# Graph network with two residual layers on one core: another order of the preparation, fewer rows gathered ahead, and other queues and store sizes in the last stage

## The reference

```python
msg_in = concat([x[src], edge_attr], -1)             # 400,000 x 192
h = relu(msg_in @ W1.T + b1)
messages = h @ W2.T + b2
agg = segment_sum(messages, dst)                     # 12,500 x 128
# a GRU cell with agg as its input and x as its state
r, z = sigmoid(i_r + h_r), sigmoid(i_z + h_z)
n = tanh(i_n + r * h_n)
x = layernorm(x + (1 - z) * n + z * x)
# second layer: mean over the edges in the other direction
agg = segment_sum(x[dst], src);  deg = segment_sum(1, src)
x = layernorm(x + agg / max(deg, 1) @ weight + x @ root_weight + bias)
```

## Time and profile before

| | us |
|---|---|
| median of 3 runs | 4435.34 (4431.68 to 4440.71) |
| the profiled execution | 4442.85 |
| its span | 4441.0 |
| PE busy | 3928.3 (88%) |
| POOL busy | 3013.7 (68%) |
| DVE busy | 2906.7 (65%) |
| ACT busy | 2353.3 (53%) |

### The profile page before, as it was taken

One profiled execution on the slowest core, in us unless ns is written; L12 is line 12 of the kernel. 1 busy time (PEld: TensorE's weight loads), 2 busy tenths in 40 slices (PEclk: granted clock), 3 DMA queues, 4 the chain that ended last, 5 costly groups with the idle time before them and its releaser, 6 DMA issues.

```text
span 4441.0 us, 106931 instructions
## 1 busy us (share of the span) xinstructions
PE 3928.3 (88%) x39936; PEld 3633.4 (82%) x39936; DVE 2906.7 (65%) x7270; ACT 2353.3 (53%) x4278; POOL 3013.7 (68%) x3198
## 2 busy tenths in 40 slices
PE   6488999988989898999999998989898999989875
PEld 6377888887979797988888897979797888879775
DVE  4465667666666676666666666667676676766644
ACT  2165555555555555555555555555555555555633
POOL 1677777777777777777777777777777777777600
PEclk9587999999999999989999998999999999999989
DMA  7455888797969697978879796969798887979655
GB/s 216 87 173 159 231 232 248 219 260 212 268 192 287 200 272 212 254 218 235 242 221 257 216 269 194 283 199 277 212 257 225 234 242 224 265 211 273 193 169 167
DMA packets 1017822, 999.82 MB, mean 225 GB/s; under 512 B 204167, under 2 KB 857548, under 8 KB 1016921
## 3 DMA queue, kind: packets, MB, share of 16 engines
q1 hardware_dynamic: 830878, 459.88, 40.3%
q10 hardware_dynamic: 84075, 321.56, 21.2%
q0 software_dynamic: 102352, 211.43, 18.4%
HBM read 655.22 MB, written 337.22 MB: 223 GB/s over the span
## 4 chain that ended last, share of the span: by engine, by line
PE 69%; DMA 7%; DVE 7%; ACT 4%; issue 3%; SPq 3%; POOL 2%; DVEq 1%; ACTq 0%; POOLq 0%
PE stream_pse L1193 15%; PE stream_psa L1202 13%; PE stream_pse L1185 13%; PE stream_psw L1209 10%; PE stream_psw L1208 10%; DMA ring<-in_ea_blocks_dram 5%; PE stream_psw L1246 2%; ACT stream_a_sb L893 2%; SPq L749 2%; PE stream_psw L1247 2%; POOL ring L838 2%; PE stream_psw L1248 2%; DVE stream_col L978 1%; ACT stream_hid L855 1%; DMA ring<-r 1%
## 5 line engine op out<-in xcount | busy, mean ns | idle before, releaser
L838 POOL DMA_INDIRECT ring<-y,ring x2480 | 2349.6, 947 | 842.9 <-issue 728.9
L893 ACT CAST stream_a_sb<-stream_psa 98x512 f16<-98x512 f32 x3125 | 1770.5, 586 | 1508.5 <-PE stream_psa L1202 1468.2
L1202 PE MATMUL stream_psa<-stream_col,stream_row 128*98 128x256 f16 x6250 | 1145.2, 284 | 157.2 <-ACT stream_a_sb L893 125.8
L1208 PE MATMUL stream_psw<-stream_z,stream_strip 128*128 128x129 f16 x9060 | 1255.3, 221 | 14.1 <-issue 6.9
L1209 PE MATMUL stream_psw<-stream_z,stream_strip 128*128 128x128 f16 x9060 | 1260.9, 221 | 0.0
L1193 PE MATMUL stream_pse<-w1b,ring 128*128 128x128 f32 x6250 | 1037.2, 300 | 79.1 <-DVE stream_tiny L1105 32.7
L956 DVE TENSOR_TENSOR ring<-stream_pse,ring 128x384 f32<-128x384 f32 x1000 | 489.3, 489 | 830.4 <-PE stream_pse L1193 745.9
L978 DVE TENSOR_TENSOR stream_col<-stream_ramp,stream_twin 128x1536 f16<-128x1536 f16 x1250 | 1019.7, 816 | 0.0
L1193 PEld LDWEIGHTS stream_pse<-w1b,ring 128*128 128x128 f32 x6250 | 869.3, 205 | 124.0 <-DMA ring<-in_ea_blocks_dram 36.0
L1208 PEld LDWEIGHTS stream_psw<-stream_z,stream_strip 128*128 128x128 f16 x9060 | 889.7, 98 | 19.8 <-issue 12.0
L1209 PEld LDWEIGHTS stream_psw<-stream_z,stream_strip 128*128 128x128 f16 x9060 | 887.8, 98 | 21.5
(11 more groups left out here) (201 smaller groups left out, 2014.4 us busy)
## 6 DMA issues: line engine op xcount, KB each, us to landing
A<-stream_a_sb ACTq DMA_DIRECT2D x625, 490.0 KB
stream_strip<-A SPq DMA_DIRECT2D x1862, 160.0 KB
ring<-in_ea_blocks_dram SPq DMA_DIRECT2D x625, 160.0 KB
ring<-y,ring POOLq DMA_INDIRECT x2500
stream_yg<-y,ring POOLq DMA_INDIRECT x625
stream_col<-A SPq DMA_DIRECT2D x84, 96.0 KB, 2.5
prologue_xt<-in_xT_dram SPq DMA_DIRECT2D x14, 448.0 KB, 4.4
y<-prologue_ysb SPq DMA_DIRECT2D x14, 448.0 KB, 3.1
```

Of the source, the lines that this page charges most:

```text
L838: nc.gpsimd.indirect_dma_start(out=yg[s.c % YR][:, t, :], out_offset=None, in_=h.y, in_offset=bass.IndirectOffsetOnAxis(ap=idx[s.c // (PH ...
L893: nc.scalar.copy(a_sb[s.c % AR][0:RW, j, :], psa[BANK[j]][0:RW, :]).then_inc(a_out, 1)
L1202: last = nc.tensor.matmul(psa[BANK[j]][0:RW, e * LOS:(e + 1) * LOS], row1[s.c % 2][:, 2 * j + e, :], col1[s.c % 2][:, 2 * j + e, :], start ...
L1208: nc.tensor.matmul(bank[:, e * (P + 1):(e + 1) * (P + 1)], a, b[:, 0:P + 1], start=(n == 0), stop=False)
```

## The change

- **Order of the prologue.** The samples are loaded first, and the one-hot tables of the first two parts are made before the edge codes. Two counts stand right behind `y(0)`. Of the 14 `y(k)`, four stand among the code turnings (at the pairs 0, 2, 5 and 7, `Y_AFTER`), the other ten between the window turnings. `segment_keys`, `block_places` and `folded_weights` come after the key parts 2, 5 and 11. The two large loads `dcol` and `dbase` are issued later.
- **Queues and buffers.** `E` is stored from SP's queue and from three buffers `ek`. The weights are loaded behind the stores of `E`. The padding of `A` is stored one piece at a key part.
- **Layout of `y`.** Tile j of a step is 128 neighbouring columns of `xt`, so TensorE reads them side by side, and each row of `y` is stored by a run of 512 bytes, where 7 rows made a run of 3,584 bytes.
- **Gathers ahead.** One block of edges is gathered in `prologue` instead of four (`AHEAD = 1`).
- **The last stage.** `load_r` is issued from POOL's queue. SP stores two strips by one transfer.

The helper functions that stand out of the diff (`count`, `turn_codes`, `keys` and others) are as before.

```diff
+EK = 3
+Y_AFTER = [0, 2, 5, 7]
+AHEAD = 1
...
+            def load_x(k):
                 if k >= 2:
                     sp.wait_ge(y_ready, 2 * (k - 1))
-                sp.dma_start(xt[k % 2][:], h.xT[:, k * TC:(k + 1) * TC]).then_inc(xt_in[k % 2], 16)
...
+            def store_y(k):
+                sp.wait_ge(y_out, 2 * k + 2)
+                sp.dma_start(h.y_rows[k], ysb[k % 2][:]).then_inc(y_stored[k % 2], 16)
+
+            def store_e(n):
+                sp.wait_ge(e_out, n + 1)
+                for x, t in enumerate(pair_tiles(n)):
+                    r = LASTQ if t == QS - 1 else P
+                    sp.dma_start(h.E_rows[t * P:t * P + r], ek[n % EK][0:r, x].rearrange("p (j q) s -> p j (q s)", j=4)
+                                 ).then_inc(e_stored[n % EK], 16)
+
+            load_x(0)
+            sp.wait_ge(src_in, 64)
+            load_x(1)
+            for n in range(EP):
+                store_e(n)
+                if n in Y_AFTER:
+                    k = Y_AFTER.index(n)
+                    store_y(k)
+                    load_x(k + 2)
+            sp.wait_ge(w1b_zero, 1)
+            sp.dma_start(h.w1b[DE:DE + 1], h.b1).then_inc(kept_in, 16)
+            for to, data in h.weights:
+                sp.dma_start(to, data).then_inc(kept_in, 16)
+            for tile, data in ((w2[:], h.w2), (b2[:], h.b2), (bih[:], h.bih), (bhh[:], h.bhh), (wih[:], h.wihT)):
+                sp.dma_start(tile, data).then_inc(given, 16)
             sp.wait_ge(counted, 4)
...
+            for k in range(len(Y_AFTER), NC):
+                store_y(k)
+                load_x(k + 2)
...
+            act.dma_start(samp[:, 0:SAMP], h.samples).then_inc(samples_in, 16)
+            act.dma_start(samp[:, SAMP:S2], h.dst_keys[FINE:FINE + 1, 0:KW].rearrange("a (s c) -> (a s) c", c=SAMP)).then_inc(samples_in, 16)
...
+            y_copy(0)
+            act.wait_ge(lo_int, 1)
+            nc.scalar.copy(lo, src4[:]).then_inc(lo_ready, 1)
+            act.dma_start(dcol[:], h.dst_col).then_inc(dst_col_in, 16)
+            act.dma_start(dbase[:], h.dst_first.partition_broadcast(P)).then_inc(dst_col_in, 16)
...
+            for n in range(EP):
+                e_copy(n)
+                if n in Y_AFTER[1:]:
+                    y_copy(Y_AFTER.index(n))
...
+                if q + len(Y_AFTER) < NC:
+                    y_copy(q + len(Y_AFTER))
+                for k, x in pads[q:q + 1]:
+                    act.dma_start(h.A[1][k * C:(k + 1) * C, (GB * BLOCKS - AG) * LOS + x * ZC:(GB * BLOCKS - AG) * LOS + (x + 1) * ZC], zero[:]).then_inc(pad_stored, 16)
...
-            for c in range(4):
+            for c in range(AHEAD):
...
+            sample_digits()
+            for q in range(2):
+                onehots_of(q)
             edge_codes()
-            sample_onehots()
+            for q in range(2, 4):
+                onehots_of(q)
             histogram()
-            segment_keys()
             running_sum()
-            block_places()
             first_edges()
             window_rows()
             for q in range(QUADS):
                 keys(q)
                 if q == 2:
+                    segment_keys()
+                if q == 5:
+                    block_places()
+                if q == QUADS - 2:
                     folded_weights()
             verdict()
...
-                                                xt[k % 2][:, j::NT], w1a[:], start=True, stop=True)
+                                                xt[k % 2][:, j * P:(j + 1) * P], w1a[:], start=True, stop=True)
...
             pe.wait_ge(masks, 7)
+            for q in range(2):
+                count(q)
             pe.wait_ge(c1_ready, 1)
             pe.wait_ge(lo_ready, 1)
...
+            for n in range(EP):
+                turn_codes(n)
+                if n == 2:
+                    count(2)
+                if n == 6:
...
+                if n in Y_AFTER[1:]:
+                    y(Y_AFTER.index(n))
...
+                if q + len(Y_AFTER) < NC:
+                    y(q + len(Y_AFTER))
+                if q == QUADS - 3:
+                    pe.wait_ge(given, 80)
+                    pe.wait_ge(y_out, 2 * NC)
+                    nc.tensor.matmul(psy[0][:, 0:3 * D], w2[:], wih[:], start=True, stop=True).then_inc(made, 1)
+                    nc.tensor.matmul(psy[1][0:1, 0:3 * D], b2[:], wih[:], start=True, stop=True).then_inc(made, 1)
...
-            def load_r(c):
-                if c >= 2:
-                    sp.wait_ge(o_ready, 2 * (c - 1))
-                if c == (ITER + 1) * PN // LOS:
-                    sp.wait_ge(r_stored, 16 * (ITER + 2) + 1)
-                sp.dma_start(rr[c % 2], h.r[c * LOS:(c + 1) * LOS, :].rearrange("(e p) f -> p e f", e=2)).then_inc(r_in[c % 2], 16)
-
-            def store_out(c):
-                sp.wait_ge(out_ready, 2 * c + 2)
-                sp.dma_start(h.out[c * LOS:(c + 1) * LOS, :].rearrange("(e p) f -> p e f", e=2), out[c % 4]
-                             ).then_inc(out_stored[c % 4], 16)
+            def store_out(n, strips):
+                sp.wait_ge(out_ready, 4 * n + 2 * strips)
+                sp.dma_start(h.out[2 * n * LOS:(2 * n + strips) * LOS, :].rearrange("(e p) f -> p e f", p=P),
+                             pair[n % 2][:, 0:2 * strips, :]).then_inc(out_stored[n % 2], 16)
 
             for c in range(RING - 1):
                 load_late(c)
-            sp.wait_ge(r_stored, 16 * (ITER + 1) + 1)
-            for c in range(2):
-                load_r(c)
...
-                if c + 2 < C:
-                    load_r(c + 2)
-                if c >= 3:
-                    store_out(c - 3)
-            for c in range(C - 3, C):
-                store_out(c)
-            for x in range(4):
-                sp.wait_ge(out_stored[x], 16 * ((C + 3 - x) // 4))
+                if c >= 4 and c % 2 == 0:
+                    store_out(c // 2 - 2, 2)
+            store_out(C // 2 - 1, 2)
+            store_out(C // 2, 1)
+            for x in range(2):
+                sp.wait_ge(out_stored[x], 16 * ((C // 2 + 2 - x) // 2))
 
         @block.gpsimd
...
-                if s.c < 4:
+                if s.c < AHEAD:
...
+            def load_r(c):
+                if c >= 2:
+                    pool.wait_ge(o_ready, 2 * (c - 1))
+                if c == (ITER + 1) * PN // LOS:
+                    pool.wait_ge(r_stored, 16 * (ITER + 2) + 1)
+                pool.dma_start(rr[c % 2], h.r[c * LOS:(c + 1) * LOS, :].rearrange("(e p) f -> p e f", e=2)).then_inc(r_in[c % 2], 16)
+
+            pool.wait_ge(relu_done, BLOCKS)
+            pool.wait_ge(r_stored, 16 * (ITER + 1) + 1)
+            for c in range(C):
+                load_r(c)
 
...
-        h.y_rows = h.y.rearrange("(k p j) d -> k p j d", p=P, j=WB)
+        h.y_rows = h.y.rearrange("(k j p) d -> k p j d", p=P, j=WB)
```

112 lines of the change are left out of this document (35 added, 77 removed).

## The result

The changed kernel takes 4370.28 us (median of 4 runs, 4353.99 to 4379.15) against 4433.51 of the kernel before in the same comparison (4 runs, 4425.14 to 4440.71): a ratio of 0.9849, interval 0.9829 to 0.9868 (the two medians alone divide to 0.9857). The forecast was 4360, with a range of 4338 to 4398. The profiled execution has a span of 4377.4 us, 63.6 less than that of the earlier trace rows; like that one it is slower than its median, by 8.9 us.

A forecast was written before the change was run, and what follows sets the result against it. POOL's gathers bound the start, TensorE most of the chain and SP's queue the last stage. Start 43 plus last stage 32 gave 75 us off the median 4435.3, so 4360 us, range 4338 to 4398.

The forecast's parts named there:

- start 43: Prologue to `stream`: 31 us from an earlier first row gather plus 12 from fifteen gathers fewer before the barrier.
- Window gathers at 64, gain 26: Prologue: POOL's first window gather comes at 64 us instead of 90.0, decided by `E`; bounds 58 and 72.
- My count by buffers: Stores of `E`: three buffers `ek` give 2.04 us a pair, so 13 pairs end at 58 and have landed at 62.
- The windows themselves, 4 us over 61.3: Prologue: 49 window gathers take 61.3 us, plus 4 for transfers, bounds 0 and 12; first row gather at 129.3.
- the ring of two quads hides: Windows phase: `segment_keys` (8 us) delays VectorE by 3 us against a quad's 5.0, hidden; uncovered it costs those 3.
- Fifteen gathers fewer, 17 us from first row gather to block 1, gain 12: Before the barrier: block 1 starts 17 us after the first row gather instead of 28.8; ends 14.5 and 31.7.
- The last stage, 3.25 us a strip: Last stage: SP's queue sets the pace, strips 3.25 us apart instead of 4.0, gaining 32 us over 42 rounds.
- The rival in which `r` becomes the bound: Last stage: `r` through POOL sets 3.65 us a strip, sum 58 us, time 4377 us; chance 0.11.
- `y` products of half the time: Prologue, TensorE: contiguous weight loads take 143 ns instead of 327, so `y` products take about half today's time.
- The edits cancel: Whole kernel within 0.2% (9 us): barrier waits for degree store, windows slow (13 in sum), `r` dear or worse; chance 0.02.
- dear end: Last stage: slow bound for `r` through POOL, up to 3.65 us a strip, leaving a gain of 15 us.
- The slower rival: Last stage: POOL's `r` loads starve as VectorE shuts POOL out; at 5.8 us a strip, 4468 us; chance 0.03.

The follow-up runs named there:

- run 9: The changed kernel with `segment_keys` and `block_places` moved ahead of the first keys and five buffers for `E` instead of three; ratio to the kernel before 0.9834.
- Run 4: The changed kernel with `segment_keys` and `block_places` moved up, behind `window_rows` and ahead of the first keys; ratio to the kernel before 0.981.
- run 1: The kernel before with one block of rows gathered in the prologue instead of four; ratio to the kernel before 0.9996.
- run 5: The changed kernel with two blocks gathered ahead instead of one; ratio to the kernel before 0.9866.
- runs 7 and 8: The kernel before with only the output stores paired (ratio 0.9974), and the kernel before with only the loads of `r` moved to POOL's queue (ratio 0.9938).
- run 12: The changed kernel with `segment_keys` and `block_places` moved ahead of the first keys and the old layout of `y`; ratio to the kernel before 0.9842.

## Why the prediction was right, and where it was off

- **The sum**: start 43 and last stage 32, in all 75. Measured in the profiled execution: start 39.7, of which 32.0 are left at the last stage's first strip load, last stage 32.4, in sum 64.4 and a span shorter by 63.6. Each of the two parts of the start is further off than the start itself: the first row gather gains 22.7 instead of 31, the gathers fewer 17.1 instead of 12. That the start came within 3.3 us of 43 is in part luck. The forecast's "the shift stays through `stream`" is off by 7.8 us in these two executions, which is within their spread.
- **Window gathers at 64, gain 26**: measured 66.2, gain 23.8. That `E` decides and not `at` was right (`at` at 51.95, forecast 54). My count by buffers was beside the point: with five of them (run 9) the windows start no earlier. The last store of `E` is issued by 60.3 us where I had 58, and 5.9 more pass to the first window, of which I had 4.2 for the landing and the rest in "a few us for DMA traffic".
- **The windows themselves, 4 us over 61.3**: measured 10.7. This is the step that failed. I wrote that the work of `segment_keys` delays VectorE and "the ring of two quads hides" it. VectorE's delay is hidden; but the long instructions hold POOL itself. Run 4 gives 66.0 us without them, 4.7 over, near the 4 that I had for transfers. (The 282 GB/s of that term should be 288, since its KB are of 1,024 bytes; the changed kernel moved 305 and 327 GB/s from 80 to 90 us, above the 298 that I took as the best mix.) In the kernel before they cost nothing, since POOL was waiting then.
- **Fifteen gathers fewer, 17 us from first row gather to block 1, gain 12**: measured 11.7, gain 17.1. Here I weighed the right mechanism, a gather held by the degree store, and took a value between its two cases. Nothing between was seen: all five gathers were ahead of the store by 0.69 us (11.7), while in run 1 one stood behind it by 0.11 (24.0). The measured 11.7 even lies below my near end of 14.5: that took 8.2 us for the crossing from an execution whose last gathers stood behind the store, and with all ahead of it the crossing is 5.4. I forecast one gather behind the store; that none was is luck of order for the forecast, though it repeats (0.69 to 1.45 us ahead in the six runs with the new prologue and one block ahead). `AHEAD = 2` (run 5) falls into the other case.
- **The last stage, 3.25 us a strip**: measured 3.23, and runs 7 and 8 confirm that it is SP's issuing. I had 0.33 to 0.47 a strip for the paired store; it is 0.30. The rival in which `r` becomes the bound did not come: its issue is 0.71 us, its landing 3.7, and VectorE waits 2.4 us in all. On its two parts see runs 7 and 8.
- **`y` products of half the time**: their weight loads take 192 ns instead of 327, not 143. I took nothing for TensorE being held up by them, and run 12 puts what the layout is worth at 0 to 3 us.
- **The edits cancel**: this rival's own sum doesn't reach its 9 us. Windows at their slow end (13) and `r` at its dear end (15) make 28, so it needed an `r` far worse than the dear end. No run came near it.
- **The slower rival** (VectorE shuts POOL out) named the real mechanism but in the wrong place: it showed at the window gathers, not at `r`. I had set it aside because the gathers of `stream` are steady, and they are, where VectorE's instructions with two SBUF inputs average 0.95 us at most. That their length is the reason is not shown.

## What to carry to other kernels

Before work is moved beside an engine that was waiting, ask what else the moved instructions hold: VectorE instructions of 3.4 us beside gathers issued by GpSimd were not free here even where VectorE had time. A transfer of many tiny runs delays whatever is issued after it, so count which transfers stand on which side of it, above all ahead of a barrier; a fraction of a microsecond decided 12 us here. Where a queue's issue times fill its round, a transfer taken out of that queue pays its issue, until another limit is reached, and one transfer of two pieces can cost the issue of one.

## What the runs showed of the hardware

- Two window gathers grew from 0.94 to 4.46 and 3.84 us beside VectorE instructions of 3.40 us (L437) and 3.42 us (L444), each with two SBUF inputs. They ended 1.13 and 0.81 us behind the end of these instructions, which is about the time of a gather by itself. L442 between them, 0.98 us with one SBUF input, need not have held anything, though the first gather also ends 0.12 us behind it. The Trainium skill, "SBUF — State Buffer", SBUF: two separate sides, says that a VectorE instruction with two SBUF inputs and a GpSimd instruction that reads SBUF exclude each other, and that the later one is blocked for the whole instruction of the earlier; the trace agrees here. It does not agree in `stream`: there VectorE has two instructions with two SBUF inputs, of 948 and 683 ns, in every block (L1006), and 2,495 gathers still average 947 ns, the longest 1.50 us. Which property of the instruction or of its timing decides stays open.
- The degree store, 49 KB in runs of 8 bytes, takes 20.0 to 25.4 us to land and fills the DMA engines (share 1.92) at 3 GB/s. Rows gathered behind it were first used 1.0 to 1.1 us behind its landing in six runs.
- The barrier between the blocks opens 5.4 us behind POOL's last gather where all gathers stand ahead of the degree store or the store is away (seven runs), and 18.0 and 20.6 us behind it where one gather or a few stand behind the store (runs 1 and 5).
- A load of `r` with 256 runs from POOL's queue costs 0.71 us of issue, less than a gather of 128 rows (0.94).
- SP's issue of an output store takes 467 ns behind a load of `r` and 599 ns behind strip loads, the same for 256 runs of 512 bytes as for 512.
